# Weights laid out on the host, a shorter start, and constant products for TensorE in a recurrent + MoE + attention kernel

## The reference

```python
x = x + _L0_xcond_ref(_layernorm(x, axis=-1), cond_1024, ctx_1024, ...)   # the recurrence
x = x + _L0_ffn_ref(_layernorm(x, axis=-1), ...)                          # 64 experts, top 8, and a shared one
x = x + _L1_xcond_ref(_layernorm(x, axis=-1), ...)                        # two attentions (16 heads), feed-forward
x = x + _L1_ffn_ref(x, ...)

def step(carry, x):                       # of the recurrence, per batch
    h, stopped = carry
    stop = jnp.logical_or(stopped, jnp.mean(x) == 0)
    logits = jnp.concatenate([x, h]) @ W_attn.T + b_attn
    applied = softmax(logits) @ enc
    comb = relu(jnp.concatenate([x, applied]) @ W_comb.T + b_comb)
    h_new = jnp.tanh(comb @ W_ih.T + b_ih + h @ W_hh.T + b_hh)
    out = h_new @ W_out.T + b_out         # zero once stopped
```

## Time and profile before

| | us |
|---|---|
| median of three runs | 999.96 (999.63 to 1000.25) |
| profiled execution | 994.99 |
| its span, first to last instruction | 993.1 |
| TensorE busy | 894.8 |
| VectorE busy | 723.8 |
| GpSimd busy | 586.6 |
| ScalarE busy | 479.9 |

### The profile page before, as it was taken

How to read it: one execution, slowest core, us unless ns; L and a number is a source line. 1 busy time by engine, 2 the same in 40 slices (tenths; PEclk the granted TensorE clock), 3 DMA queues, 4 the chain that set the end, 5 groups by cost and what they waited for, 6 DMA issues and landing times. The chain is left out here.

```text
span 993.1 us, 32236 instructions
## 1 busy us (share of the span) xinstructions
PE 894.8 (90%) x13470; PEld 719.0 (72%) x13470; DVE 723.8 (73%) x1818; ACT 479.9 (48%) x899; POOL 586.6 (59%) x648
## 2 busy tenths in 40 slices
PE   3489558999999999999999997999999999998886
PEld 3377546778878887778887875778787878786554
DVE  5676675876867677676769665878888878878665
ACT  2234323323232322323232225888788888887752
POOL 3588842435443434444366655867786877776773
PEclk9655556999999999999999997999999999999997
DMA  9212008342222322222233420000000000000001
GB/s 255 53 24 60 22 1 163 99 108 79 87 68 66 86 68 68 71 81 68 79 97 106 117 78 1 3 3 3 3 3 4 3 3 3 3 3 2 3 1 43
DMA packets 46531, 51.82 MB, mean 52 GB/s; under 512 B 22163, under 2 KB 37300, under 8 KB 46388
## 3 DMA queue, kind: packets, MB, share of 16 engines
q1 hardware_dynamic: 43472, 48.78, 18.7%
q10 hardware_dynamic: 2916, 1.01, 0.6%
HBM read 48.20 MB, written 1.57 MB: 50 GB/s over the span
## 5 line engine op out<-in xcount | busy, mean ns | idle before, releaser
L770 POOL TENSOR_TENSOR ex<-ex,xn 128x256 f32<-128x256 f32 x256 | 184.1, 740 | 216.4 <-DVEq L1477 104.8
L1911 PE MATMUL ps<-ex,wd 128*128 128x256 f32 x512 | 140.6, 398 | 0.6 <-DVE xT L1464 0.6
L1024 ACT ACTIVATE thcb<-ps 128x512 f32<-128x512 f32 x132 | 77.5, 597 | 78.3 <-PE ps L1876 68.9
L1449 DVE SCALAR_TENSOR_TENSOR ex<-thcb,ps 128x512 f32<-128x512 f32 x132 | 90.6, 687 | 26.1 <-ACT thcb L1024 18.8
L852 POOL TENSOR_TENSOR wd<-wd,a_sum 128x512 f32<-128x512 f32 x64 | 66.7, 1044 | 69.2 <-DVE a_sum L1582 69.0
L1876 PE MATMUL ps<-xnT,wu 128*128 128x256 f16 x768 | 106.0, 275 | 0.0
L1876 PE MATMUL ps<-xnT,wg 128*128 128x256 f16 x768 | 105.8, 274 | 0.3 <-DVE ex L1449 0.2
L858 POOL TENSOR_TENSOR wu<-encC,wu 128x1024 f16<-128x1024 f32 x44 | 93.7, 2145 | 12.6 <-ACT encC L1106 12.6
L1969 PE MATMUL ps<-wg,M 128*128 128x128 f16 x1536 | 97.6, 221 | 2.0 <-DVE wg L1551 2.0
L1969 PEld LDWEIGHTS ps<-wg,M 128*128 128x128 f16 x1536 | 92.4, 99 | 6.8 <-DVE wg L1551 2.4
L1823 PEld LDWEIGHTS ps<-eb,encC 128*128 128x128 f16 x3072 | 86.7, 98 | 14.1 <-DVE eb L1321 7.3
(11 more groups left out here) (338 smaller groups left out, 1847.9 us busy)
## 6 DMA issues: line engine op xcount, KB each, us to landing
xn<-coef_rows SPq DMA_DIRECT2D x128, 256.0 KB, 3.9
thcb<-in_L_ffn_Wg SPq DMA_DIRECT2D x8, 256.0 KB, 3.3
thcb<-in_L_ffn_Wu SPq DMA_DIRECT2D x8, 256.0 KB, 3.4
wd<-in_L_ffn_Wd SPq DMA_DIRECT2D x2, 1024.0 KB, 10.2
xtok<-in_x SPq DMA_DIRECT2D x4, 256.0 KB, 5.8
thcb<-in_ctx SPq DMA_DIRECT2D x2, 512.0 KB, 10.9
wu<-in_L_xcond_attn_wq SPq DMA_DIRECT2D x2, 512.0 KB, 11.0
wu<-in_L_xcond_attn_wk SPq DMA_DIRECT2D x2, 512.0 KB, 10.6
```

The source lines that it names most:

```text
L770: nc.gpsimd.tensor_tensor(hid[:, side(m, n), own], gu[:, side(m, n), own], other[:, own], ALU.mult)\
L1024: nc.scalar.activation(th[:, side(m, n), :], bank(side(m, n)), ACT.Tanh, scale=0.5 / WSCALE)\
L1449: V.scalar_tensor_tensor(ga[:, :], th[:, side(m, n), :], 1.0, bank(side(m, n)), add, mul)\
L1911: last = mm(bank(5)[:, half * HT:(half + 1) * HT], wd[:, 2 * q + p, :], hid[:, side(m, n), p * HT:(p + 1) * HT], start=(n == 0 and p == 0) ...
```

## The change

- The host lays out the inputs (transposed and joined, no arithmetic): x by tile, the context transposed, all weights of the recurrence in one array `w_all`, attention weights by head. The transposes of weights and context go, and their DMAs become few, with rows of 2 KB and more.
- Of x, VectorE treats only the first 4 tiles ahead of the steps. GpSimd does sums, centring and squares of the other 12; their scans and normalisation stand in VectorE's gaps 3 to 22 (`REST`), their transposes in gaps 20, 24 and 27. The root is refined on GpSimd.
- The exact steps: chunk 0 and 8 of chunk 1 ahead of GpSimd's gaps, 9 more in gaps 40 to 49, those of chunks 2 and 3 in halves of 256 columns, one behind each of the first 68 expert units (`EXACT_AT`).
- The stop flags of chunks 1 to 3 move from chunk 0 into their own chunk; chunk 0's moves from gap 14 to gap 31.
- The folded weights are plain f32 products, four per group, eight pairs in gaps 28 to 56; the splits of expert weights move to gaps 15 to 78.
- `coef_wide` has a buffer of its own; `wd` is loaded from ScalarE's queue at gap 56; the loads of feed-forward weights move to chunk 3.
- `keep_busy`: in the first 16 steps TensorE multiplies the constant `wx` with itself into bank 5 (128x256 f16), five times (once where a set-up group follows) after the logits and twice after the hidden-state product where no x products follow. Nothing reads it.

```diff
+            groups.append(("ctx_in", [(i * P, ("m", ctxT[:, (4 * g + i) * P:(4 * g + i + 1) * P], w_T[:, 1, :]))
+                                      for i in range(4)],
+                           tuple(encC[:, x, 4 * g:4 * g + 4, :] for x in range(2))))
+
+        def xn_group(g):
+            return ("xn_ready", [(i * P, tr(xn[:, 4 * g + i, :])) for i in range(4)],
+                    tuple(xnT[:, g * 512:(g + 1) * 512].bitcast(F16).rearrange("p (x a b) -> p x a b", x=2, b=P)[:, x]
+                          for x in range(2)))
+
+        groups.append(xn_group(0))
...
+        groups.append(("norm_in", [(j * B, ("m", norm_w[:, j // 2, (j % 2) * P:(j % 2 + 1) * P], condT)) for j in range(6)],
+                       ss[:, :, :].rearrange("p a b -> p (a b)")))
+        for g in range(1, CH):
+            groups.append(xn_group(g))
         paired = set()
-        while transposes:
-            groups.extend(transposes[:2])
-            n_wvT = len(groups) - 1
-            transposes, now, products = transposes[2:], products[:2], products[2:]
-            paired.add(len(groups))
-            groups.extend(now)
-        n_folded = len(groups)
-        groups.extend(products)
-        for a in range(2):
-            for g in range(4):
-                heads = range(8 * (g // 2) + g % 2, 8 * (g // 2) + 8, 2)
-                groups.append(("o_lo", [((h % 8 // 2) * P, ("h", wvT[64 * (h % 2):64 * (h % 2) + 64, a, :, h // 2, :],
-                                                      o_pieces[2 * a + h // 8][64 * (h % 2):64 * (h % 2) + 64, :, h % 8 // 2, :]))
-                                         for h in heads],
-                               tuple(N[a][:, x, heads[0]:heads[0] + 7:2, :] for x in range(2)), n_wvT))
+        for what, left_w, right_w, folded in (("qk_in", qT, kT, M), ("vo_in", vT, wo, N)):
+            for a in range(2):
+                for g in range(4):
+                    if g % 2 == 0:
+                        paired.add(len(groups))
+                    heads = range(8 * (g // 2) + g % 2, 8 * (g // 2) + 8, 2)
...
+                    r = slice(64 * (g % 2), 64 * (g % 2) + 64)
+                    groups.append((what, [((h % 8 // 2) * P, ("m", left_w[r, a, h // 2, :], right_w[r, a, h // 2, :])) for h in heads],
+                                   tuple(folded[a][:, x, heads[0]:heads[0] + 7:2, :] for x in range(2))))
...
+        LATE = {12: n_norm, 20: N_RNN + 1, 24: N_RNN + 2, 27: N_RNN + 3}
+        LATE.update({28 + 4 * i: N_FOLD + 2 * i for i in range(8)})
...
+        SPLITS = {4 * c + (15 if c <= SHARED else 14): c for c in range(WEIGHTS)}
...
+        EXACT_NOW = 2
+        STOPS = {31: ("scan0", 0), 32: ("scan1", 0), 33: ("flags", 0), 34: ("sum", 0), 36: ("count", 0), 37: ("keep", 0), 16: ("scales", 0)}
+        for m in range(1, CH):
+            at_ = GAPS * m + (6, 14, 18)[m - 1]
+            STOPS.update({at_: ("scan0", m), at_ + 4: ("scan1", m), at_ + 5: ("flags", m),
+                          at_ + 6: ("sum", m), at_ + 7: ("count", m), at_ + 9: ("keep", m)})
+        COUNT = slice(2 * P, 2 * P + NT)
+        REST = {3: ("scan", 1), 5: ("scan", 2), 7: ("scan", 3), 10: ("eff", 0), 14: ("normal", 1), 18: ("normal", 2), 22: ("normal", 3)}
...
+        STEPS = 17
+        EXACT_LATE = 8
+        EXACT_AT = {gap: EXACT_LATE + i for i, gap in enumerate((40, 41, 42, 43, 45, 46, 47, 48, 49))}
+        EXACT_AT.update({gap: STEPS + i for i, gap in enumerate(sorted(PASS_AT)[:4 * STEPS])})
...
+            sp.dma_start(xtok[:, 0:TPC, :].rearrange("p n d -> p (n d)"), ins["x"][:, 0:CT]).then_inc(s["x_in"], 16)
+            sp.dma_start(w_all[:, :], ins["rnn_w"]).then_inc(s["rnn_w_in"], 16)
+            sp.dma_start(xtok[:, TPC:NT, :].rearrange("p n d -> p (n d)"), ins["x"][:, CT:CH * CT]).then_inc(s["x_rest_in"], 16)
+
+            for w in range(4):
+                sp.dma_start(wu_f[:, w * H * DH:(w + 1) * H * DH], ins["att_w"][w]).then_inc(s["qk_in"], 16)
+            for w in range(4):
+                sp.dma_start(wd_flat[:, w * H * DH:(w + 1) * H * DH], ins["att_w"][4 + w]).then_inc(s["vo_in"], 16)
+            sp.dma_start(swd[:, :], ins["swd"]).then_inc(s["moe_w_in"], 16)
...
-            sp.wait_ge(s["exact_ready"], CH * 17)
-            sp.wait_ge(s["setup_ps"], N_RNN)
             for m in range(CH):
                 coef_pass(m, 0)
-                if first(m):
+                if m == CH - 1:
...
+            root(slice(0, TPC), 1)
+
+            pool.wait_ge(s["x_rest_in"], 16)
+            late = slice(TPC, NT)
+            TT = nc.gpsimd.tensor_tensor
+            settle(TT(lanes[:, late, :], xtok[:, late, 0:16], xtok[:, late, 16:32], ALU.add))
...
+            for c in range(1, CH):
+                r = slice(c * TPC, (c + 1) * TPC)
+                settle(TT(cen[:, r, :], xtok[:, r, :], mean[:, r].unsqueeze(2).broadcast_to([P, TPC, P]), ALU.subtract))
+                TT(xn[:, r, :], cen[:, r, :], cen[:, r, :], ALU.mult).then_inc(s["sq_ready"], 1)
...
+            tables = [exact_table(c * TPC, TPC, tuple(ex[:, i, :].rearrange("p (n d) -> p n d", d=P) for i in range(1, 7)))
+                      for c in range(EXACT_NOW)]
+            for i in range(STEPS):
+                exact(tables[0], i, 0)
+            step_sums()
...
+            for i in range(EXACT_LATE):
+                exact(tables[1], i, STEPS)
...
+                if at in EXACT_AT:
+                    done, i = divmod(EXACT_AT[at], STEPS)
+                    exact(tables[1 + done], i, (1 + done) * STEPS)
...
+            for half in range(2):
+                act.dma_start(ctxT[:, half * B * L // 2:(half + 1) * B * L // 2],
+                              ins["ctxT"][:, half * B * L // 2:(half + 1) * B * L // 2]).then_inc(s["ctx_in"], 16)
+            act.dma_start(b_rows[:, :], ins["rows"]).then_inc(s["rows_in"], 16)
+            act.dma_start(ebias[:, :], ins["e_bias"].partition_broadcast(P)).then_inc(s["norm_in"], 16)
+            act.dma_start(cols_in[:, :], ins["cols"]).then_inc(s["norm_in"], 16)
...
+                    if g == N_SETUP - 1:
+                        act.dma_start(wd_flat, ins["wd"]).then_inc(s["moe_w_in"], 16)
...
+            dve.wait_ge(s["x_in"], 16)
+            settle(V.tensor_tensor(lanes[:, head, :], xtok[:, head, 0:16], xtok[:, head, 16:32], add))
...
+            def rest(p, c):
+                if p == "scan":
+                    dve.wait_ge(s["sq_ready"], c)
+                    last = V.tensor_tensor_scan(rest_scan[:, c * CT:(c + 1) * CT], blockmask[:, :], xn_flat[:, c * CT:(c + 1) * CT],
+                                                0.0, mul, add)
+                    if c < CH - 1:
+                        settle(last)
+                    else:
+                        last.then_inc(s["den0_ready"], 1)
+                elif p == "normal":
+                    if c == 1:
+                        dve.wait_ge(s["den0_ready"], 4)
+                        settle(V.reciprocal(rden[:, TPC:NT], den[:, TPC:NT]))
+                    normal(c)
...
-                        for i, (u, v) in enumerate(HALVES):
-                            last = mm(setup_bank(g)[:, col:col + P], l0[:, u, :], r0[:, v, :], start=(i == 0), stop=(i == 2))
-                            last2 = mm(setup_bank(g + 1)[:, col2:col2 + P], l1[:, u, :], r1[:, v, :], start=(i == 0), stop=(i == 2))
+                        last = mm(setup_bank(g)[:, col:col + P], l0, r0, start=True, stop=True)
+                        last2 = mm(setup_bank(g + 1)[:, col2:col2 + P], l1, r1, start=True, stop=True)
...
+            def keep_busy(times):
+                for _ in range(times):
+                    mm(bank(5)[:, 0:2 * P], wx[:, 0, :], wx[:, :, :].rearrange("p x d -> p (x d)"), start=True, stop=True)
...
+                    if first(chunk):
+                        keep_busy(5 if 4 * st not in LATE else 1)
...
+                    elif first(chunk):
+                        keep_busy(2)
...
+    laid = {
...
+        "x": x.reshape(B, T // 4, 4, D).transpose(2, 0, 1, 3).reshape(P, -1),
+        "ctxT": named("ctx_1024").reshape(-1, D).T,
...
+        "att_w": np.stack([by_head(named(f"{a}_{w}").T) for a in att for w in ("wq", "wk")]
+                          + [by_head(named(f"{a}_wv").T) for a in att] + [by_head(named(f"{a}_wo")) for a in att]),
```

More of the change, by code:

```diff
@@ L51, in build @@
 def build(nc, ins, out):
-    B, T, D = ins["x"].shape
-    L = ins["ctx_1024"].shape[1]
-    E, _, I = ins["L0_ffn_Wg"].shape
+    B, T, D = out.shape
+    L = ins["ctxT"].shape[1] // B
+    I = ins["swd"].shape[0] // 2
+    E = ins["wg"].shape[1] // I
     TL = P // B
@@ L292, in landed @@
         def landed(eng, c):
-            eng.wait_ge(s[f"landed{slot_of(c)}"], 16 * sum(1 + (i == SHARED) for i in range(c + 1) if slot_of(i) == slot_of(c)))
+            eng.wait_ge(s[f"landed{slot_of(c)}"], 16 * sum(slot_of(i) == slot_of(c) for i in range(c + 1)))
         def landing_view(c):
@@ L651, in coef_pass @@
```

(26 more changed lines are left out.)

529 lines of the change are left out of this document (222 added, 307 removed).

## The result

The changed kernel takes 983.85 us (median of 4, 982.92 to 984.88) against 999.80 in the same session: ratio 0.9852, 95% interval 0.9819 to 0.9886. The forecast was 968.2 (950 to 985): the sign and the range held, but of the 31.8 us forecast 16 came. The profiled execution took 982.92 us, 981.1 of it span, 12.0 less than the profile before: the kernel before took 994.7 to 997.3 us in a few of its executions and 999.6 to 1001.8 in most, and its profile is one of the few.

What follows compares the result with a forecast made beforehand. It took start-up to wait for VectorE, the sixteen steps to be a chain through four engines, and steps 16 to 63 to keep TensorE busy. -25.6 - 10.2 + 4 = -31.8 us gave 968.2 us, range 950 to 985.

Steps and rivals of the forecast that it cites:

- Start-up: Up to the first softmax exp: it comes at 18.0 us (16.5 to 20.5) instead of 43.6, -25.6 us.
- Sixteen steps: First sixteen recurrence steps: 104.3 us against 114.5, -10.2 us.
- rival 3: Chunks 1 and 2: every exact step lands before a VectorE instruction that the chain waits for; 1014 us, chance 0.03.
- the flag scan: Sixteen steps: chunk 0's flag scan comes in, +4.4 us.
- The constant products: Sixteen steps: they fit in TensorE's waits, priced at 0 (bounds 0 and 0.2 us per step), without lifting the clock.
- GpSimd: Chunk 0: its exact work is done at 58.5 us, 2 us before VectorE wants it at gap 31.
- Rival 2: Folded weights: the f32 pairs run one after another, 8 x 2 us more, 984 us; chance 0.15.
- Steps 16 to 63: Third stage: exact steps and flag scans beside the expert units cost +4 us, bounds -2 and +20.
- Last stage: Attention and feed-forward behind the recurrence: the change leaves it alone, 0 us.
- The 5 us carried: Whole kernel: the median lies 5.0 us above the profiled execution, as before the change; 963.2 becomes 968.2 us.

Runs made afterwards that it cites:

- experiment 1: Changed kernel with the seven operations on ss moved back from step 4 to step 18, as in the kernel before: 974.16 us, ratio 0.9742.
- the pairs: Versions of the changed kernel without and with the constant products: 979.89 and 983.85 us; with further edits in both, 971.79 and 973.80, 971.39 and 974.04.
- the first profile: Profiled execution of the changed kernel, 982.92 us; the second is of the same kernel measured again beside other versions, median 983.51 us.
- experiment 4: Changed kernel with the feed-forward weight loads issued ahead of the last chunk's first coefficient pass, not between its two passes: 977.02 us, ratio 0.9782.

## Why the prediction was wrong

- **Start-up** (-25.6, measured -24.5): right within its bounds, with terms off against each other. x's head landed at 7.03 us, not 3.8: the queues moved 9 GB/s to 2 us, 186 from 2 to 4 and 297 from 4 to 7, with 1 MB of context in them beside x; it wasn't the 400 that I took from a later stretch; ctxT came at 10.05. VectorE's work and the root went as priced. xn's head was written by 15.59 us in place of 12.1, the comb products ran to 15.96, and the transposes of xn ended at 16.4, where the forecast had 14.4. From there to the first exp it took 2.8 us in place of 3.6.
- **Sixteen steps** (-10.2, measured -0.6): this is the step that failed. The sum leaves out an edit: seven operations on ss, moved into step 4, put at nothing because they aren't in the sum at all; they made that step 13.1 us long, and 5.9 without them. With ss away chunk 0 takes 104.3 us. The mechanism was even named, in rival 3 and the earlier trace rows, at the wrong place. The profiled span missed by 19.8 us: 1.1 in the start-up, 9.6 here, 5.7 in steps 16 to 63, 3.4 behind them; the median missed by 15.7, as 4.1 were won back by the last point below.
- That the sum without ss came out is in part luck. Its terms give steps 0 to 6 and 15 some 44 us and steps 7 to 14, with pairs, flags and routing, some 60; experiment 1 has 51.2 and 53.1. The five steps without a set-up group take 6.7, 5.8, 5.3, 5.9 and 6.2 us, not 5.2, and the flag scan, priced at 4.4 us, ran there as two of 0.70 and 0.67 us.
- **The constant products**: clock right (no lasting rise), price too low. They were put at 0 (up to 0.2 us per step, 3 in all); the pairs have chunk 0 1.2 to 1.4 us longer, 0.4 to 0.9 of it in the first step, within that bound, and the medians 2 to 4 us.
- **GpSimd** keeps up, as forecast: chunk 0's exact chain ended at 62.9 us (forecast 58.5; 17 x 1.45 is 24.7, not 24.2), and the scan at 77.0 didn't wait for it. Rival 2 (f32 pairs one after the other) falls: a pair's 16 products took 2.07 us (69.74 to 71.81), near the 1.75 that I counted.
- **Steps 16 to 63** (+4, measured +9.7, bounds -2 to 20): the price was put on the wrong item. The exact operations cost under 1 us by the profile, the flags 6 us in chunks 2 and 3 together with the clock falls behind them. Chunk 1 lost 3.1 us in the first profile and 0.9 in the second, most of it to a later rise of the clock, which no term held. Before, these flags ran in chunk 0; now nmax stands right behind them.
- **Last stage** (0, measured +3.4): a queue that I didn't follow. SyncE's loads were moved ahead of a store (2.05 us by experiment 4); the rest goes with falls of the clock.
- The 5 us carried from the profiled execution to the median were too much: the changed kernel's median is 0.9 above its profiled execution. This offset 4.1 us of the misses, by luck. In which stage the kernel before spends its 5 us no trace shows.

Open: what sets the moments at which the clock rises behind step 16, and why it fell three times in the tail of some versions and not of others with the same instructions. Versions with the same instructions in a stretch differ there by 2 to 5 us, as much as many of the differences above; step 4, the flags of chunks 2 and 3, and the 2.05 us of the loads (five times) stand clear of it. Not tried: moving chunk 0's norm product, which step 3 (7.8 us) still pays for.

## What to carry to other kernels

List every entry of a schedule that changed its slot, however small, and price it where it lands. Small VectorE operations on SBUF tiles (additions, tensor_scalar) took their own time where GpSimd was idle and one GpSimd operation each beside a stream of long ones, so count operations, merge them, and look at GpSimd's row before calling a VectorE wait a cover. Follow each DMA queue in program order, and ask what a moved load now stands in front of.

## What was unexpected in the hardware

- Seven short VectorE operations beside GpSimd's exact chain took 7.3 us where they take 1.8 alone; three on the same data 3.3 us.
- Beside the earlier trace rows, one more fall of the clock without a long wait ahead of it: from 289 to 294.2 us TensorE was busy 3.05 of 5.2 us and idle at most 2.15 us in one piece. The Trainium skill, TensorE: Matmul & The Clock Gate, HAM oscillation, puts the throttle's return down to longer idle gaps; these rows don't agree, nor do.
- The level isn't cheap to hold: 121 constant products in place of 60 raised the mean granted clock of the sixteen steps from 0.52 to 0.56 and made them 2.4 us longer.
